# Modulation columns, the first x load, the last z projection and filler products on TensorE, in an AdaLN block of a state-space mixer and a routed transformer layer

## Chip, core and metric

The kernel runs on one core of a Trainium2 chip. The metric is the device time of one execution in microseconds (us); the time before is the median of three runs, 1469.33 us. Engines are named as in the profile: PE is TensorE, ACT is ScalarE, DVE is VectorE, POOL is GpSimd, SP is SyncE, which issues the plain DMAs.

## What is computed

```python
mod = (silu(c) @ wmod).reshape(8, 6, 1, 256)     # sa, ca, ga, sb, cb, gb
h = layernorm(x) * (1 + ca) + sa                 # x: 8 x 1024 x 256
x = x + ga * mixer(h)
h = layernorm(x) * (1 + cb) + sb
x = x + gb * ffn(h)

def mixer(u):                                    # inner width 512, 8 heads, state 64
    x = silu(causal_conv4(u @ Wx.T)); z = u @ Wz.T
    b, c = x @ Wb.T, x @ Wc.T; dt = softplus(x @ Wdt.T + b_dt)
    y = scan(x, b, c, dt, -exp(log_a)) + d * x   # state recurrence over 1024 tokens
    return (groupnorm(y) * silu(z)) @ Wout.T     # z is first needed here

def ffn(x):                                      # 127 of 1024 tokens, picked by a router
    attention (16 heads) and a GELU MLP on the picked tokens, scattered back
```

ga and gb are also clamped away from zero.

## The kernel before, in words

Eight batches run one after the other, all in float32 but for a few bfloat16 operands. Each engine has its own program, written out by hand; it works through it in order and meets the others at semaphores. The mixer of batch b and the routed layer of batch b-1 are interleaved in `batch(b, f)` with f = b-1; the last batch's routed layer (f = 7) follows alone, with nothing to interleave. That stretch, from the end of the last scan to the end of the kernel, is called the tail.

Within a batch PE does: `ln_in` (transposes of the normalised x), `x_proj` and `z_proj` (8 calls each, two halves of 512 tokens by four column blocks, each call two products of 512 columns that the trace shows as 4 records), `bc_proj`, `dt_proj`, then `scan` over eight chunks, whose last product group is `output`. The results go through a ring `proj` of four PSUM banks: job q uses bank q % 4 and waits until job q-4 has been read. `gn_stats`, `out_` and the `ffn_...` steps of batch f stand between them: `ffn_wrow` waits for the router weights `wcol` of DVE, `ffn_rank` for DVE's comparisons, `ffn_idx` for DVE's one-hot rows (`ffn_onehot`), `ffn_turn` for the gathered and normalised tokens, `ffn_AT` for the softmax.

On DVE `out_(f)` (residual, statistics, `wcol`) comes first in a batch, then the convolution in four pieces with `ffn_rank` and `ffn_onehot` between them. On ACT `gn_apply` scales y, `z_silu` writes silu(z), and DVE multiplies the two before PE's `out_` can begin.

At the start SP loads cT and the first 512 columns of wmod, then all of x of batch 0, the rest of wmod and the weights. PE makes row-wise modulation (`modulation(0)`), ACT copies it out, DVE adds 1 to ca, PE turns it into columns (L1489) and ACT copies them into `mcol`; `modulation(1)` and `(2)` follow. The normalised x (ACT L653) waits behind these copies on ACT, and PE's first `x_proj` waits for x and the columns.

The tail on PE before:

```python
output(f, T - 1)
gn_stats(f)
out_(f)
ffn_wrow(f)
ffn_rank(f)
ffn_idx(f)
```

Of the kernel before, what the change touches and what calls it, by code (L numbers as in the profile page):

```python
# [20 lines left out]
ACT = mybir.ActivationFunctionType  # L21
AX = mybir.AxisListType

P = 128
# [19 lines left out]
SD_MOD, SD_MIX, SD_ALL = 10, 12, 16  # L44
# [34 lines left out]
class Ring:  # L79
# [3 lines left out]
    def __init__(self, banks, filled, drained):  # L83
        self.banks, self.filled, self.drained = banks, filled, drained
# [3 lines left out]

    def full(self, b, q):

        return self.filled[q % 4], at(self.filled[q % 4], b, q // 4 + 1)

    def read(self, b, q):

        return self.drained[q % 4], at(self.drained[q % 4], b, q // 4 + 1)


def adaln_block(nc, x, wxT, wzT, wbT, wcT, wdtT, woT, cols, bdt, loga, mask, pos, rw, rb,
                wqkv, wo, w1, w2, lncols, cT, wmod, out):
    ctx = ExitStack()  # L100
    with ctx:
# [175 lines left out]
        mload = ctx.enter_context(nc.semaphore("mod_inputs_loaded"))  # L277
# [86 lines left out]
        def ring(name, banks, jobs):  # L364
            return Ring(banks, [sig(f"{name}_filled{i}", len(range(i, jobs, 4))) for i in range(4)],
                        [sig(f"{name}_drained{i}", len(range(i, jobs, 4))) for i in range(4)])

        proj = ring("proj", ps[0:4], 49)
# [3 lines left out]
        J_X = ((4, 2, 6, 7), (8, 9, 10, 11))  # L372
        J_BC = ((20, 21, 22, 23, 24, 25, 26, 27), (29, 31, 33, 34, 35, 36, 39, 40))
# [8 lines left out]
        def kp(w):  # L382
            return w.rearrange("(k p) n -> p k n", p=P)

        first_loads = ((bdt_s[:, :], bdt), (arow[:, :], loga.partition_broadcast(P)), (cols_s[:, :, :], cols), (wx_s[:, :, :], kp(wxT)),
                       (wz_s[:, :, :], kp(wzT)))
# [7 lines left out]
        def _(sp):  # L394


            sp.dma_start(mcin, cT.rearrange("(k p) n -> p k n", p=P)).then_inc(mload, 16)
            sp.dma_start(wmod_s[:, :, 0:2 * D], kp(wmod)[:, :, 0:2 * D]).then_inc(mload, 16)
            sp.dma_start(xin[:, :, :], x[0, :, :].rearrange("(t p) n -> p t n", p=P)).then_inc(x_loaded, 16)
# [9 lines left out]
            sp.dma_start(mod_d[:, :], mod8).then_inc(mod_stored, 16)  # L409
# [48 lines left out]
        def _(pool):  # L458
# [8 lines left out]
            def ln_in(b, half):  # L467
# [22 lines left out]
                                 base=0, pattern=[[0, 4], [1, P]], channel_multiplier=-1))  # L490
            link(g.memset(ones_b[:, :], 1.0))
# [10 lines left out]
                        allow_small_or_imprecise_dtypes=True))  # L502
            link(g.memset(above[:, :], 0.0))
# [17 lines left out]
            ln_in(0, 0)  # L521
            ln_in(0, 1)
# [113 lines left out]
        def _(act):  # L636
            a = nc.scalar

            act.wait_ge(mload, 16 * 2)
            a.activation(mcin, mcin, ACT.Silu).then_inc(setup_act, 1)  # L640
            act.wait_ge(setup_pe, 1)
            a.activation(mod8[:, 0:2 * D], ps[4][0:NB, :], ACT.Copy).then_inc(setup_act, 1)
            act.wait_ge(setup_pe, 2)
            a.activation(mcol[:, :, :], ps[7][:, 0:4 * NB].rearrange("p (a n) -> p a n", a=4), ACT.Copy
                         ).then_inc(setup_act, 1)
            for j in (1, 2):
                act.wait_ge(setup_pe, j + 2)
                a.activation(mod8[:, 2 * j * D:2 * (j + 1) * D], ps[4 + j][0:NB, :], ACT.Copy).then_inc(setup_act, 1)
# [16 lines left out]
            def gn_apply(b):  # L665
                act.wait_ge(gcoef_ready, at(gcoef_ready, b, 1))
                for half in range(2):
# [38 lines left out]
            def z_silu(b, half, pair):  # L706
                for m in (2 * pair, 2 * pair + 1):
                    q = J_Z + half * KC + m
# [141 lines left out]
            def batch(b, f, last=False):  # L850
                x_copies(b, ((0, (0, 1)),))
                ln_rows(b, 1)
                x_copies(b, ((0, (2, 3)), (1, (0,))))
# [3 lines left out]
                if f is None:  # L857
                    act.wait_ge(mod_stored, 16)
                    act.wait_ge(setup_pool, SP_ALL)
                last_tap(b, 0)  # L860
                z_silu(b, 0, 0)
                z_silu(b, 0, 1)
                last_tap(b, 1)
                z_silu(b, 1, 0)
# [3 lines left out]
                z_silu(b, 1, 1)  # L868
                x_silu(b, 0, 1)
                if f is not None:  # L870
                    second_norm(f)
                bc_copies(b, 0, (0, 1, 2, 3, 4))
# [601 lines left out]
        def _(pe):  # L1474
# [20 lines left out]
            def ln_in(b, half):  # L1495
# [6 lines left out]
                for k in range(KD):  # L1502
                    q = J_H[half][k]
                    if q >= 4:
                        pe.wait_ge(*proj.read(b, q - 4))
# [472 lines left out]
```

## Time and profile before

| | |
|---|---|
| median of 3 runs (lowest, highest) | 1469.33 us (1468.57, 1469.62) |
| the profiled execution, its own time | 1468.33 us |
| its span | 1466.3 us |
| PE busy | 1372.3 us, 94% |
| DVE busy | 996.5 us, 68% |
| ACT busy | 689.5 us, 47% |
| POOL busy | 308.7 us, 21% |
| share of PE in the chain that ended last | 87% |
| mean granted clock of PE | 0.977 |

The span is the profile's own window; the execution's time is 2.0 us more. A busy PE means that matmuls are in flight, not that they run at full speed. The granted clock is 1.00 at 2.4 GHz and 0.50 at 1.2 GHz. The two ends of the kernel are where PE is not busy: over the first 20 us and over the tail, some 115 us long.

### The profile page before, as it was taken

Reading aid. Unit: us, or ns where it says so; the run is one execution under the profiler, and the core shown is the slowest. Engines: PE = TensorE matmul, PEld = TensorE weight load, DVE = VectorE, ACT = ScalarE, POOL = GpSimd, SP = SyncE. Lnnn points to the kernel's source line nnn. Section 1 sums busy time; section 2 is a strip of 40 time slices with the busy share of each in tenths; the row PEclk is TensorE's granted clock in tenths of the full one; section 3 lists DMA queues with packets and bytes.
Section 4 is the critical chain, followed back from the end, with each engine's and each line's share of the span. In section 5 each row is a group of like instructions: output and inputs, shape, how many; then the busy total and the mean of one; then the engine's idle time right before and its main releaser. Section 6 shows DMA issues by size and latency. Waiting matters only on the chain.

```text
span 1466.3 us, 23175 instructions
## 1 busy us (share of the span) xinstructions
PE 1372.3 (94%) x8656; PEld 849.5 (58%) x8656; DVE 996.5 (68%) x2848; ACT 689.5 (47%) x1353; POOL 308.7 (21%) x386
## 2 busy tenths in 40 slices
PE   7999999999999999999999999999999999998434
PEld 2447655676457665576456764576655764567423
DVE  2426797477874787477974778747874779747782
ACT  4434543645445462635436454555626354362212
POOL 3004201241104301142013411043011420133110
PEclk9999999999999999999999999999999999999767
DMA  8001001020000200020010200001000200101010
GB/s 302 6 0 30 15 15 47 3 75 29 25 23 10 68 30 26 22 77 15 15 47 3 76 30 26 22 20 59 29 26 22 77 15 15 47 4 45 29 47 4
DMA packets 47534, 54.24 MB, mean 37 GB/s; under 512 B 7608, under 2 KB 42296, under 8 KB 47424
## 3 DMA queue, kind: packets, MB, share of 16 engines
q1 hardware_dynamic: 41408, 46.42, 9.4%
q0 software_dynamic: 6016, 6.35, 1.7%
q8 instruction: 69, 1.13, 0.3%
q14 instruction: 41, 0.34, 0.1%
HBM read 34.84 MB, written 17.87 MB: 36 GB/s over the span
## 4 chain that ended last, share of the span: by engine, by line
PE 87%; DVE 6%; issue 3%; ACT 1%; DMA 1%; POOL 1%; POOLq 0%; SPq 0%; DVEq 0%; ACTq 0%
PE ps L1519 43%; PE ps L1684 8%; PE ps L1634 5%; PE ps L1593 4%; PE ps L1586 4%; DVE yst L1130 3%; PE ps L1646 2%; PE ps L1605 2%; PE ps L1824 2%; PE ps L1834 2%; PE ps L1620 2%; PE ps L1624 1%; PE ps L1611 1%; PE ps L1789 1%; PE ps L1755 1%
## 5 line engine op out<-in xcount | busy, mean ns | idle before, releaser
L1519 PE MATMUL ps<-xT,wb_s 128*128 128x512 f32 x512 | 230.9, 597 | 0.1
L1519 PE MATMUL ps<-xT,wc_s 128*128 128x512 f32 x512 | 225.4, 593 | 0.0
L1519 PEld LDWEIGHTS ps<-xT,wc_s 128*128 128x128 f32 x512 | 96.1, 190 | 112.3 <-issue 111.9
L1519 PEld LDWEIGHTS ps<-xT,wb_s 128*128 128x128 f32 x512 | 93.6, 190 | 108.4 <-issue 100.9
L1011 DVE SCALAR_TENSOR_TENSOR xT<-xc,cols_s,xT 128x512 f32<-128x512 f32 x192 | 134.8, 748 | 3.2 <-ACT xT L697 0.6
L1519 PE MATMUL ps<-hT,wx_s 128*128 128x512 f32 x256 | 119.0, 609 | 1.9 <-ACT hT L662 1.5
L1684 PE MATMUL ps<-CT,xT 128*128 128x256 f32 x512 | 114.0, 384 | 6.3 <-DVE xT L1190 6.3
L1519 PE MATMUL ps<-hT,wz_s 128*128 128x512 f32 x256 | 112.3, 592 | 0.0
L1684 PEld LDWEIGHTS ps<-CT,xT 128*128 128x128 f32 x512 | 98.7, 193 | 23.2 <-issue 9.8
L729 ACT ACTIVATE BT<-ps 128x512 f32<-128x512 f32 x64 | 37.9, 593 | 151.2 <-PE ps L1519 151.2
L770 ACT ACTIVATE XB<-ps 128x512 f32<-128x512 f32 x64 | 38.4, 599 | 138.3 <-PE ps L1605 138.3
L759 ACT ACTIVATE Eg<-ps 128x512 f32<-128x512 f32 x128 | 72.6, 596 | 53.1 <-PE ps L1624 43.3
L729 ACT ACTIVATE CT<-ps 128x512 f32<-128x512 f32 x64 | 38.1, 595 | 124.3 <-PE ps L1519 124.3
L1113 DVE TENSOR_TENSOR Sbd<-ps,Sdc 64x256 f32<-64x256 f32 x96 | 40.5, 421 | 67.2 <-PE ps L1593 66.5
L603 POOL TENSOR_TENSOR sm<-sm,mhalf 128x1 f32<-128x1 f32 x24 | 14.4, 599 | 324.1 <-DVE sm L1398 307.3
L1099 DVE TENSOR_TENSOR Mt<-ps,Eg 128x512 f32<-128x512 f32 x128 | 82.1, 683 | 0.0
L546 POOL TENSOR_TENSOR EC<-EC,CT 128x512 f32<-128x512 f32 x64 | 79.7, 1272 | 1.3
L1519 PEld LDWEIGHTS ps<-hT,wz_s 128*128 128x128 f32 x256 | 48.1, 190 | 54.9 <-issue 54.5
L1519 PEld LDWEIGHTS ps<-hT,wx_s 128*128 128x128 f32 x256 | 46.9, 192 | 53.3 <-issue 50.6
L552 POOL TENSOR_TENSOR Sdc<-Sbd,dec 128x512 f32<-128x512 f32 x48 | 50.4, 1049 | 127.4 <-DVE Sbd L1113 108.6
L1406 DVE TENSOR_TENSOR ftmp<-ftmp,ps 128x256 f32<-128x256 f32 x8 | 3.4, 420 | 108.6 <-PE ps L1834 108.6
L1634 PE MATMUL ps<-CT,BT 64*128 64x128 f32 x1024 | 74.4, 285 | 1.6 <-ACT EC L749 1.6
(298 smaller groups left out, 2589.0 us busy)
## 6 DMA issues: line engine op xcount, KB each, us to landing
BT<-x SPq DMA_DIRECT2D x8, 1024.0 KB, 5.5
xr<-x SPq DMA_DIRECT2D x8, 1024.0 KB, 9.2
x_scratch<-xr SPq DMA_DIRECT2D x32, 256.0 KB, 2.1
out<-EC SPq DMA_DIRECT2D x32, 256.0 KB, 2.1
modrow<-mod_scratch SPq DMA_DIRECT2D x8, 512.0 KB, 6.8
w_s<-w SPq DMA_DIRECT2D x2, 1024.0 KB, 12.4
xT<-wmod SPq DMA_DIRECT2D x1, 1024.0 KB, 8.6
wb_s<-wbT SPq DMA_DIRECT2D x1, 1024.0 KB, 10.6
```

The lines of the kernel that those rows point to most:

```text
L546: g.tensor_tensor(s, s, CT[:, half, k, :], ALU.mult).then_inc(CE_ready, 1)
L552: g.tensor_tensor(Sdc[:, :, :], Sbd[:, :, :], dec[:, :, c:c + 1].broadcast_to([P, KC, P]), ALU.mult).then_inc(Sdc_ready, 1)
L729: a.activation((BT if m < KC else CT)[:, half, m % KC, :], proj.bank(q)[:, :], ACT.Copy).then_inc(proj.drained[q % 4], 1)
L759: a.activation(Eg[:, s * HALF:(s + 1) * HALF], ps[s][:, :], ACT.Exp).then_inc(Eg_ready, 1)
L1011: ins = v.scalar_tensor_tensor(dst, xcv[:, m, half * HALF + tap:half * HALF + tap + HALF], cols_s[:, m, tap:tap + 1], dst, ALU.mult, ALU.add)
L1099: v.tensor_tensor(Mt[:, c % 2, s * HALF:(s + 1) * HALF], ps[2 + s][:, :], Eg[:, s * HALF:(s + 1) * HALF], ALU.mult).then_inc(Mt_ready, 1)
L1130: ins = v.bn_stats(yst[:, k, 6 * part:6 * part + 6], xT[:, k, first * P:end * P])
L1519: ins = t_.matmul(bank[:, :], w[:, k, m * P:(m + 1) * P], rhs[:, k, half * HALF:(half + 1) * HALF], start=k == 0, stop=k == nk - 1)
L1586: t_.matmul(ps[4][:, k * P:(k + 1) * P], Sbd[:, k, :], ECv[:, k, c * P:(c + 1) * P], start=k == 0, stop=True, skip_group_check=k > 0)
L1593: ins = t_.matmul(ps[4][64 * hh:64 * hh + 64, k * P:(k + 1) * P], XB[:, c % 2, 0, h * STATE:(h + 1) * STATE], Mt[:, c % 2, hh * HALF + k * ...
L1634: ins = t_.matmul(ps[2 + s][:, k * P:(k + 1) * P], BT[r, c // 4, k, chunk(c)], CT[r, c // 4, k, chunk(c)], start=True, stop=True)
L1684: ins = t_.matmul(ps[4 + j][:, i * D:(i + 1) * D], xT[:, k, t * P:(t + 1) * P], wog_s[:, k, :], start=k == 0, stop=k == KC - 1)
```

## The change

There are four edits. At the start, x's first half (512 KB) is the first load and x's second half comes after wmod's first part; the modulation columns are made by PE directly in column form and read by DVE, and `modulation(1)` and `(2)` move behind the fourth `x_proj` call; the exponential of log_a on ACT moves behind the `x_copies`; POOL's two `ln_in` stand earlier in its setup. In the last batch (b = 7) all eight `z_proj` calls move behind the scan, around `gn_stats`, into ring jobs 49 to 56; ACT's `z_silu` for them stands around `gn_apply`. In the tail ACT does `ffn_wrow` ahead of `second_norm`. And `keep_busy(n)` puts n products of 512 bfloat16 columns that nobody reads into a bank of PSUM: 17 at the start, 122 in the tail.

```diff
+            sp.dma_start(xin[:, 0:4, :], x[0, 0:HALF, :].rearrange("(t p) n -> p t n", p=P)).then_inc(xhead, 16)
+            sp.dma_start(mcin, cT.rearrange("(k p) n -> p k n", p=P)).then_inc(cload, 16)
             sp.dma_start(wmod_s[:, :, 0:2 * D], kp(wmod)[:, :, 0:2 * D]).then_inc(mload, 16)
-            sp.dma_start(xin[:, :, :], x[0, :, :].rearrange("(t p) n -> p t n", p=P)).then_inc(x_loaded, 16)
+            sp.dma_start(arow[:, :], loga.partition_broadcast(P)).then_inc(aload, 16)
+            sp.dma_start(xin[:, 4:T, :], x[0, HALF:L, :].rearrange("(t p) n -> p t n", p=P)).then_inc(x_loaded, 16)
+            sp.dma_start(wx_s[:, :, :], kp(wxT)).then_inc(wxload, 16)
             sp.dma_start(wmod_s[:, :, 2 * D:], kp(wmod)[:, :, 2 * D:]).then_inc(mload2, 16)
...
-            pe.wait_ge(mload, 32)
-            pe.wait_ge(setup_act, 1)
-            modulation(0)
-            pe.wait_ge(setup_dve, 1)
-            pe.wait_ge(setup_pool, 2)
-            for j in range(4):
-                ins = t_.transpose(ps[7][:, j * NB:(j + 1) * NB], mod8[:, j * P:(j + 1) * P], ident[0:NB, 0:NB])
-            ins.then_inc(setup_pe, 1)
-            pe.wait_ge(mload2, 16)
-            modulation(1)
-            modulation(2)
+            def mod_columns():
+                pe.wait_ge(mload, 16)
+                pe.wait_ge(setup_act, 1)
+                for j in range(4):
+                    for k in range(KD):
+                        ins = t_.matmul(ps[7][:, j * NB:(j + 1) * NB], wmod_s[:, k, j * P:(j + 1) * P],
+                                        mcin[:, k, :], start=k == 0, stop=k == KD - 1)
+                ins.then_inc(setup_pe, 1)
+
+            def keep_busy(n, bank=ps[0]):
+                for _ in range(n):
+                    t_.matmul(bank[:, :], identb[:, :], causal[:, :, :].rearrange("p a n -> p (a n)"),
+                              start=True, stop=True)
...
+            pe.wait_ge(setup_pool, 9)
+            keep_busy(8, ps[3])
+            mod_columns()
+            keep_busy(6, ps[3])
+            ln_in(0, 0)
+            keep_busy(3, ps[3])
             batch(0, None)
...
             output(f, T - 1)
+            pe.wait_ge(Eg_ready, at(Eg_ready, f, 2 * T))
+            pe.wait_ge(Mt_ready, at(Mt_ready, f, 2 * T))
+            z_proj(f, 0, range(3))
             gn_stats(f)
+            z_proj(f, 0, (3,))
+            z_proj(f, 1, range(4))
             out_(f)
+            keep_busy(12)
             ffn_wrow(f)
+            keep_busy(36)
             ffn_rank(f)
+            keep_busy(6)
             ffn_idx(f)
+            keep_busy(30)
             pe.wait_ge(hn_ready, at(hn_ready, f, 1))
...
             ffn_qT(f)
+            keep_busy(8)
             ffn_scores(f)
+            keep_busy(24)
             ffn_AT(f)
             ffn_av(f)
             ffn_wo(f)
+            keep_busy(6)
             pe.wait_ge(hnb_ready, at(hnb_ready, f, 1))
...
-            gn_apply(f)
+            z_silu(f, 0, 0)
+            z_silu(f, 0, 1)
+            z_silu(f, 1, 0)
+            gn_apply(f, (0,))
+            z_silu(f, 1, 1)
+            gn_apply(f, (1,))
+            ffn_wrow(f)
             second_norm(f)
-            ffn_wrow(f)
```

PE at the very start, before (L1478 is `modulation`, L1489 the turn into columns, L1507 `ln_in`, L1519 `x_proj`):

```order
L1478 MATMUL ps<-xT,mcin_s 8x512 x2
L1489 MATMUL ps<-ident,CT 128x8 x4
L1478 MATMUL ps<-xT,mcin_s 8x512 x4
L1507 MATMUL ps<-ident,BT 128x128 x8
L1519 MATMUL ps<-hT,wx_s 128x512 x4
```

and in the change (L1531 is `keep_busy`, L1524 `mod_columns`, L1551 `ln_in`, L1563 the projections, L1514 `modulation`):

```order
L1531 MATMUL ps<-causal,identb 128x512 x8
L1524 MATMUL ps<-mcin_s,xT 128x8 x8
L1531 MATMUL ps<-causal,identb 128x512 x6
L1551 MATMUL ps<-ident,BT 128x128 x8
L1531 MATMUL ps<-causal,identb 128x512 x3
L1563 MATMUL ps<-hT,wx_s 128x512 x4
L1551 MATMUL ps<-ident,BT 128x128 x8
L1563 MATMUL ps<-hT,wx_s 128x512 x4
L1514 MATMUL ps<-xT,mcin_s 8x512 x4
```

The four wide row products have moved from ahead of the first projection to between its calls. PE in the last batch, before, from `out_` (L1684) on:

```order
L1684 MATMUL ps<-CT,xT 128x256 x32
L1519 MATMUL ps<-hT,wz_s 128x512 x12
L1696 MATMUL ps<-ident,wcol 128x128 x8
L1519 MATMUL ps<-hT,wz_s 128x512 x4
L1519 MATMUL ps<-xT,wb_s 128x512 x12
```

and in the change (L1729 is `out_`, L1741 `ffn_wrow`):

```order
L1729 MATMUL ps<-CT,xT 128x256 x32
L1741 MATMUL ps<-ident,wcol 128x128 x8
L1563 MATMUL ps<-xT,wb_s 128x512 x12
```

The 16 z products (32 records) are gone from between `out_` and `bc_proj`. PE in the tail, where they went, around `gn_stats` (L1718), with the last `output` (L1637) ahead:

```order
L1637 MATMUL ps<-Mt,XB 64x128 x8
L1563 MATMUL ps<-hT,wz_s 128x512 x6
L1718 MATMUL ps<-pk,halfmean 128x8
L1563 MATMUL ps<-hT,wz_s 128x512 x10
L1729 MATMUL ps<-CT,xT 128x256 x32
L1531 MATMUL ps<-causal,identb 128x512 x12
L1741 MATMUL ps<-ident,wcol 128x128 x8
L1531 MATMUL ps<-causal,identb 128x512 x36
```

Six z products now stand ahead of `gn_stats` and ten behind it.

## Rows read from the trace of the kernel before

**Rows 1.** Timeline of the first 50 us: start, us, engine, line, operation

```profile
0.81 0.43 SPq L397 DMA_DIRECT2D mcin_s<-cT  x1
...
3.57 0.64 POOL L489 TENSOR_SCALAR_AFFINE_SELECT causal<-causal 128x512 bf16<-128x512 bf16 x1
...
5.72 3.46 PE L1478 MATMUL ps<-xT,mcin_s 128*8 128x512 f32 x4 [5.72 <-ACT mcin_s L640]
...
10.15 1.41 DVE L948 BATCH_NORM_STATS2 st<-BT 128x6 f32<-128x256 f32 x4
...
10.90 3.60 PE L1478 MATMUL ps<-xT,mcin_s 128*8 128x512 f32 x8 [0.32 <-DMA xT<-wmod]
...
13.82 0.20 POOL L476 TENSOR_TENSOR mrs<-mrs,negone 128x4 f32<-128x4 f32 x1
...
15.03 2.06 ACT L653 ACTIVATE BT<-BT,mrs,rstd 128x256 f32<-128x256 f32 x4
...
17.14 1.09 PE L1507 MATMUL ps<-ident,BT 128*128 128x128 f32 x8 [2.64 <-ACT BT L653]
...
19.45 5.23 PE L1519 MATMUL ps<-hT,wx_s 128*128 128x512 f32 x8 [1.21 <-ACT hT L662]
...
35.84 13.90 PE L1519 MATMUL ps<-hT,wz_s 128*128 128x512 f32 x32
```

**Rows 2.** PE's timeline, last batch and tail; idle before, releaser in brackets

```profile
1211.64 10.46 PE L1519 MATMUL ps<-hT,wz_s 128*128 128x512 f32 x24
...
1241.25 0.34 PE L1717 MATMUL ps<-tok,Mt 128*128 128x2 bf16 x8
...
1352.20 1.09 PE L1593 MATMUL ps<-Mt,XB 128*64 128x128 f32 x16
...
1397.78 0.53 PE L1707 MATMUL ps<-ones_b,EC 128*128 128x1 bf16 x14 [9.96 <-DVE Mt L1255]
...
1411.37 0.69 PE L1725 MATMUL ps<-ident,ftmp 128*128 128x128 f32 x2 [10.09 <-DVE ftmp L1314]
```

**Rows 3.** Windows of 2 us: lengths, busy time by engine, then granted clock (PEclk)

```profile
1356.00:1358.00 2.00, 0.00 (x0) 0.00 (x0) 1.93 (x8) 0.00 (x0) 0.00 (x0) 0.80 0.01 4
...
1370.00:1372.00 2.00, 2.00 (x9) 1.64 (x8) 0.14 (x1) 0.00 (x0) 0.00 (x0) 0.79 0.00 0
```

**Rows 4.** DMA issues of the first 60 us: KB, us to landing

```profile
xT<-wmod SPq DMA_DIRECT2D x1, 512.0 KB, 4.0
```

**Rows 5.** The chain that ended last: start, us, engine, tile, line

```profile
1199.93 11.87 PE ps L1684 x55
...
1300.41 3.72 PE ps L1824 x32
...
1313.31 0.43 PE ps L1620 x2
...
1359.59 0.61 PE ps L1673 x2
...
1366.54 16.20 PE ps L1684 x64
...
1442.94 5.28 PE ps L1824 x32
```

**Rows 6.** DVE's timeline in the last batch

```profile
1215.82 8.54 DVE L1011 SCALAR_TENSOR_TENSOR xT<-xc,cols_s,xT 128x512 f32<-128x512 f32 x12
1225.13 2.19 DVE L1246 SCALAR_TENSOR_TENSOR Mt<-Eg,wcol,tri 128x128 f32<-128x128 f32 x8 [0.77 <-ACT Eg L787]
...
1234.12 4.31 DVE L1011 SCALAR_TENSOR_TENSOR xT<-xc,cols_s,xT 128x512 f32<-128x512 f32 x6
...
1238.74 1.66 DVE L1267 TENSOR_SCALAR Mt<-iota_r,rank 128x128 f32<-128x128 f32 x8
```

**Rows 7.** ACT's timeline in the tail

```profile
1362.74 5.76 ACT L670 ACTIVATE xT<-xT,gab 128x512 f32<-128x512 f32 x8 [15.16 <-DVE gab L1184]
...
1387.55 1.05 ACT L787 ACTIVATE Eg<-ps 128x512 f32<-128x512 f32 x2
```

More of the change, by code:

```diff
@@ L361, in adaln_block, with ring @@
         scattered = sig("scattered", 16)
-        def ring(name, banks, jobs):
+        def ring(name, banks, jobs, short=0):
             return Ring(banks, [sig(f"{name}_filled{i}", len(range(i, jobs, 4))) for i in range(4)],
-                        [sig(f"{name}_drained{i}", len(range(i, jobs, 4))) for i in range(4)])
-        proj = ring("proj", ps[0:4], 49)
+                        [sig(f"{name}_drained{i}", len(range(i, jobs, 4))) for i in range(4)], short)
+        proj = ring("proj", ps[0:4], 49, short=20)
         ffn = ring("ffn", ps[4:8], 26)
@@ L372, in adaln_block, with z_job @@
         J_X = ((4, 2, 6, 7), (8, 9, 10, 11))
+        J_Z_LAST = J_EC + 8
+        def z_job(b, half, m):
+            return (J_Z_LAST if b == NB - 1 else J_Z) + half * KC + m
         J_BC = ((20, 21, 22, 23, 24, 25, 26, 27), (29, 31, 33, 34, 35, 36, 39, 40))
@@ L637, in _, with mod_rest @@
             a = nc.scalar
-            act.wait_ge(mload, 16 * 2)
+            act.wait_ge(cload, 16)
             a.activation(mcin, mcin, ACT.Silu).then_inc(setup_act, 1)
[L641 to L648, printed above, removed]
+            def mod_rest():
+                for j in (1, 2):
+                    act.wait_ge(setup_pe, j + 1)
+                    a.activation(mod8[:, 2 * j * D:2 * (j + 1) * D], ps[4 + j][0:NB, :], ACT.Copy
+                                 ).then_inc(setup_act, 1)
             def ln_apply(b, half):
@@ L663, in ln_rows, with gn_apply @@
                                  bias=mc[:, k:k + 1], scale=mc[:, 2 + k:3 + k]).then_inc(proj.drained[q % 4], 1)
-            def gn_apply(b):
+            def gn_apply(b, halves=(0, 1)):
                 act.wait_ge(gcoef_ready, at(gcoef_ready, b, 1))
-                for half in range(2):
+                for half in halves:
                     for k in range(KC):
@@ L857, in batch @@
                 if f is None:
-                    act.wait_ge(mod_stored, 16)
-                    act.wait_ge(setup_pool, SP_ALL)
+                    act.wait_ge(wload, 16 * len(first_loads))
+                    act.wait_ge(aload, 16)
+                    a.activation(arow[:, :], arow[:, :], ACT.Exp).then_inc(setup_act, 1)
                 last_tap(b, 0)
-                z_silu(b, 0, 0)
-                z_silu(b, 0, 1)
+                if not last:
+                    z_silu(b, 0, 0)
+                if not last:
+                    z_silu(b, 0, 1)
                 last_tap(b, 1)
-                z_silu(b, 1, 0)
+                if not last:
+                    z_silu(b, 1, 0)
                 x_silu(b, 0, 0)
@@ L867, in batch @@
                     ffn_wrow(f)
-                z_silu(b, 1, 1)
+                if not last:
+                    z_silu(b, 1, 1)
                 x_silu(b, 0, 1)
@@ L945, in ln_stats @@
             def ln_stats(b, tiles):
-                dve.wait_ge(x_loaded, at(x_loaded, b, 16))
+                if not later(b):
+                    dve.wait_ge(xhead, 16)
+                if later(b) or tiles[0] >= 4:
+                    dve.wait_ge(x_loaded, at(x_loaded, b, 16))
                 for t in tiles:
@@ L1512, in project @@
                 if q >= 4:
[L1513 removed]
+                    pe.wait_ge(*proj.prev(b, q))
                 bank = proj.bank(q)
```

94 lines of the change are left out of this document (57 added, 37 removed).

## The prediction, made before the changed kernel was run

> **What bounds the kernel now.** I read the timeline of the first 50 us first [rows 1]. PE waits there for x and for the modulation columns: it starts the first x projection at 19.45 and is then dense for the rest of batch 0. That first group of 8 records takes 5.23 us; at the pace of the z projections (32 records in 13.90, so 0.434 each and 1.74 a call) it would take 3.5. So the clock was low there, and it is worth 1.8 us. In the middle PE is the bound, and 87% of the chain that ended last is PE. Then I read PE's timeline with its idle times [rows 2]: in the tail PE stands still before nearly every group, 9.96 us before the rank products and 10.09 before the first transposes of the gathered rows. The 2-us windows show the granted clock falling from 1.00 to 0.50 (2.4 to 1.2 GHz) around 1357, four microseconds after PE's last product of the scan ended at 1353.3, and rising only around 1371, four microseconds after it became dense again [rows 2, 3].
>
> **Start.** The first load is now 512 KB of x. The nearest row is 512 KB of wmod, landed 4.0 us after its issue [rows 4]; issued at 0.81 [rows 1], x's half lands at 4.8. From the first statistics (10.15) to the end of mrs (14.02) is 3.87 us, so ACT can normalise at 8.7; its four take 2.06, and from their end (17.10) to the first projection (19.45) there were 2.35 [rows 1]. That path gives 13.1. The other path is PE's own: fillers may start when the causal mask is made, 4.2. A filler has the form of the two in 0.43 us [rows 5], so 0.216 at 2.4 GHz and 0.43 at 1.2. PE's first four records took 3.46 in all, 0.86 each, and the next eight 3.60, 0.45 each [rows 1]: the clock starts low and has risen by 10.9. I take 8 fillers at 0.43 (to 7.7), then the 8 column products. They show as 16 records; the nearest rows are 32 records with 128 columns in 3.72 warm [rows 5], 0.116 each, so 1.9 us, or 3.7 at half clock; I take 2.5, as the clock should rise on the way. Six fillers at 0.216 end at 11.5, and transposes, ACT's two copies and a high clock take 2.0 more: 13.5. Bounds for this start: 13.1 (the ACT path) and 16.3 (columns and six fillers wholly at 1.2 GHz: 7.7+3.7+2.6, plus the 2.35 of before). I take 13.5.
>
> From there to the end of the z projections: 16 calls, half of each kind, at 1.74 (27.8), 8 transposes (0.9), and now the 8 records of `modulation` as well (3.6, [rows 1]; before they lay in the wait ahead of the start). That is 32.3, so 45.8; before it was 49.74. **Gain 3.9 us.** DMA issues and the log_a exponential with its table load (some 1.5 us on ACT behind the x copies, hidden under z projections before PE needs the first xT) I cost at 0; if that cover is short, it costs up to 0.6. The late store of the modulation rows is waited for by ACT only before the B copies, when 15 us have passed: 0.
>
> The Trainium skill, "TensorE: Matmul & The Clock Gate", section "Back-to-back issue gap", gives about 131 ns per product of 512 columns in a sustained stream; the row shows 216 for this form. By the page the six fillers would end 0.5 us sooner and the gain at the start would be 4.3, not 3.9; I go by the row.
>
> **Last batch.** 32 records, 13.9 us of PE, leave a dense stretch, but what follows needs DVE. Before, z ran from 1211.64 and the index products came at 1241.25 [rows 2]. DVE finishes `wcol` just before the convolution starts at 1215.82 [rows 6]; PE, done with `out_` at 1211.7, now waits 4.1 for it. The B projection needs xT, so the convolution: its first six operations end at 1220.1, plus ACT 0.6, and the second six at 1224.4, plus 0.6. So PE starts at 1220.7, waits again until 1225.0 in the middle of the first call, and does three calls by about 1233.8 (8 records of 0.434 each, 3.47). DVE's rank compare started at 1225.13 after a wait of 0.77 for ACT's copy of wrow; this wait goes, as ACT copies it at 1221. Everything on DVE comes 0.77 sooner, the last one-hot row at 1240.40-0.77 = 1239.6 [rows 6]. PE, through with the fourth B call at 1238, waits for it, then runs the index products at 1239.65 instead of 1241.25. **Gain 1.6 us** of 13.9; some 12 go into four new waits. If the clock is low after these waits, one call costs 1.7 more, and the last wait (1.6) covers it. The rest of the batch follows with PE and DVE in step and keeps the 1.6. Bounds 0.8 (only DVE's part) and 3.
>
> **Tail.** z call by call: three from 1353.3 (end of the last `output`, [rows 2]) to 1358.5, still ahead of `gn_stats` at 1359.59 [rows 5]. Then five: the second of them after the one for half 0, so z(1,1), ends at 1365.0, its silu at 1365.6. ACT's `gn_apply` started at 1362.74 [rows 7], now it waits behind that silu: 2.9 later, and with it `out_`. But the clock stays up: `out_` took 16.20 for 64 records, and at 0.216 a record (55 in 11.87) it takes 13.8 [rows 5], 2.4 less. Sum +0.5. ACT's wrow copies ahead of the second norm: they started at 1387.55 [rows 7], behind four tiles of the second norm; PE's transposes alone allowed them some 0.3 sooner, an estimate, -0.3. Fillers: 12, 36, 6 and 30 take 2.6, 7.8, 1.3 and 6.5 at 0.216, in a gap of 4.1 (as from `out_` to `wcol` in the last batch), 9.96, the 1.66 of the one-hot rows [rows 6] and 10.09: hidden. The groups behind them run at 2.4 GHz: 32 records of w1 took 5.28 and take 3.72 warm [rows 5], -1.6. The rank, index and transpose groups are short (the first rank rows are 14 in 0.53, [rows 2]): half of about 1.5 us, -0.7, an estimate between 0 and -1.3. From the gathered rows to the end of the softmax DVE is dense, so nothing else there counts. **Gain 2.1 us**, bounds -1 (z delays not repaid by the clock) and 3.5.
>
> **Sum.** 3.9+1.6+2.1 = 7.6. The profiled execution took 1468.33 (span 1466.3): 1460.7. The median of the runs is 1.0 higher, so 1461.7.
>
> **Rivals.** (a) The clock is low through the columns and the first projections, as it was for the first 8 records: start at 16.3, gain 1.1 there, in all 4.8, time 1464.5. For it speaks that the very first products ran at half; against, that PE is now busy from 4.2 on without a break. (b) The z move doesn't do what it is meant to: the last batch gives back nothing, as DVE's own chain holds it, and the tail loses the 2.9 without the 2.4: 7.6-1.6-2.4 = 3.6, time 1465.7. For it: 24 us of DVE work between `wcol` and the last one-hot row, 1215.8 to 1240.4, that nothing shortens; against: the 0.77 and PE's own lag of 1.0 behind the one-hot rows. (c) More is gained: the start at 13.1 with the waits of the last batch shorter and clocked high (bound 3) and the tail at its 3.5: 7.6+0.4+1.4+1.4 = 10.8, time 1458.5. (d) Slower: the fillers run at 1.2 GHz. 36 take 15.5 in the 9.96 before the rank products (+5.5), 30 take 12.9 in 10.09 (+2.8), and the gains of the high clock (1.6+0.7) are lost: 7.6-10.6 = -3.0, time 1472.3. It begins to cost when one filler takes over 0.277 (9.96/36), and decides against the change when they add more than 5.3 beside the 2.3 lost. Against: at the end of `out_` the clock was 1.00 in the trace, and the pause there is now 1.2 us where a fall took four [rows 3].
>
> For (d) the Trainium skill has a rule, in the same page, section "A second HAM failure mode: psum-queue depth-cycling": small idle times between groups of matmuls can make the clock go back and forth. The trace does not bear it out: the clock held for four microseconds of full idleness after 1353.3.
>
> **How the numbers follow.** Chances: forecast 0.50, (a) 0.16, (b) 0.14, (c) 0.12, (d) 0.08, counting under (d) milder forms. A measurement of this kernel can tell 0.2%, 2.9 us, from no change. The forecast, (a) and (c) are faster; (b) at 3.6 is just so, and I put three parts in ten of it, with one quarter of (d), at no change, and give 0.05 more to errors that I don't see: faster 0.85, same 0.10, slower 0.05. The range takes in the forecast (1459.5 to 1463.5 by itself), (a), most of (b), and (c) down to where half of it lies: 1458.0 to 1466.3.
>
> **What would show it.** First x projection at 13 to 14 in 3.5 us, not 5.2; bc projections of batch 0 from 46. In the last batch idle on PE before wrow, twice in the first B call and before the index products, 12 us in all, and DVE with no gap before the rank compare. In the tail `gn_apply` behind the third pair of silus, a granted clock of 1.00 from the scan to the rank products, and w1 in 3.7. I am wrong if PE's idle before the rank products is nil (fillers on the path), if ACT's order at the start delays xT, or if the column products take 6 us.

## The result, and the profile after

| kernel | median us | runs | lowest to highest |
| --- | --- | --- | --- |
| before | 1469.6 | 20 | 1467.5 to 1475.4 |
| changed | 1466.2 | 20 | 1463.5 to 1471.1 |

The changed kernel takes 0.9979 of the time before (95% interval 0.9971 to 0.9987): 3.1 us faster by this ratio, 3.4 by the medians, and not the 7.6 of the prediction. Its profiled execution took 1465.4 (span 1463.4), against 1468.3 before.

Below, an offset is the start of a place less the start of the same place in the first profile of the kernel before; a negative one is earlier. In the profiled execution the start came out as forecast. PE's timeline of the changed kernel, first 48 us; L1531 are the unread products, L1524 the modulation columns:

```profile
4.26 3.59 PE L1531 MATMUL ps<-causal,identb 128*128 128x512 bf16 x8 [4.26 <-POOL causal L509]
7.64 2.26 PE L1524 MATMUL ps<-mcin_s,xT 128*128 128x8 f32 x16
9.76 1.46 PE L1531 MATMUL ps<-causal,identb 128*128 128x512 bf16 x6
...
13.63 3.67 PE L1563 MATMUL ps<-hT,wx_s 128*128 128x512 f32 x8 [0.89 <-ACT hT L680]
...
32.18 14.23 PE L1563 MATMUL ps<-hT,wz_s 128*128 128x512 f32 x32
```

The first x projection starts at 13.63 in place of 19.45 [rows 1] and the bc projections at 46.25 in place of 49.57: 3.3 sooner. The first eight unread products took 0.45 each (half clock), the next six 0.24.

Some 60 us later, at the scan start of batch 0, 1.3 us of this is gone. PE's timeline before (first two rows), then after; they wait equally long for ACT:

```profile
109.89 1.77 PE L1574 MATMUL ps<-xc,spread 128*128 128x512 bf16 x4 [0.19 <-ACT EC L749]
113.22 1.16 PE L1634 MATMUL ps<-CT,BT 64*128 64x128 f32 x16 [1.57 <-ACT EC L749]
```

```profile
109.91 1.21 PE L1678 MATMUL ps<-CT,BT 64*128 64x128 f32 x16 [1.57 <-ACT EC L767]
111.05 1.03 PE L1664 MATMUL ps<-causal,identb 128*128 128x512 bf16 x2
112.02 0.61 PE L1668 MATMUL ps<-xc,Lw 64*128 64x512 bf16 x2
```

Windows of the changed kernel there; the granted clock is the third number from the end (before it was 1.00 in all of them):

```profile
108.00:110.00 2.00, 0.43 (x3) 0.14 (x3) 0.00 (x0) 1.86 (x4) 1.89 (x3) 1.00 0.00 0
110.00:112.00 2.00, 2.00 (x18) 1.01 (x18) 0.00 (x0) 0.00 (x0) 2.00 (x2) 0.72 0.03 8
112.00:114.00 2.00, 2.00 (x10) 1.55 (x10) 0.00 (x0) 1.34 (x3) 1.27 (x2) 0.50 0.00 0
```

The same idle times were followed by a low clock in the one execution and not in the other. Another 0.35 goes in batch 1, where DVE stands still between two score tiles for no wait that the profile shows ("issue"). From there to batch 7 the offset stays at -1.65 or -1.66.

```profile
251.20 0.69 DVE L1408 SCALAR_TENSOR_TENSOR EC<-ps,Sbd 128x508 f32<-128x508 f32 x1 [0.27 <-issue]
```

Last batch, PE's timeline after:

```profile
1214.16 1.97 PE L1741 MATMUL ps<-ident,wcol 128*128 128x128 f32 x8 [4.01 <-DVE wcol L1246]
1219.28 3.75 PE L1563 MATMUL ps<-xT,wb_s 128*128 128x512 f32 x4 [3.16 <-ACT xT L722]
1223.42 8.94 PE L1563 MATMUL ps<-xT,wb_s 128*128 128x512 f32 x20 [0.38 <-ACT xT L722]
...
1237.94 0.35 PE L1762 MATMUL ps<-tok,Mt 128*128 128x2 bf16 x8 [1.16 <-DVE Mt L1303]
```

The four waits are where they were expected, 8.7 us in all. Of the other 5.2 of the 13.9 moved, 1.65 was gained, and most of the remaining 3.5 went into products at half clock (eight wrow records in 1.97, before 1.04; four B records in 3.75, warm 1.88). DVE's rank compare follows the convolution without a gap, as forecast. The index products stand at 1237.94 against 1241.25 [rows 2]: 3.31, less the 1.66 brought along, is 1.65.

The tail, PE's timeline after:

```profile
1349.91 5.42 PE L1563 MATMUL ps<-hT,wz_s 128*128 128x512 f32 x12
...
1366.25 14.05 PE L1729 MATMUL ps<-CT,xT 128*128 128x256 f32 x64 [0.89 <-DVE xT L1226]
...
1395.26 0.50 PE L1752 MATMUL ps<-ones_b,EC 128*128 128x1 bf16 x14 [2.09 <-DVE Mt L1291]
...
1408.77 0.69 PE L1770 MATMUL ps<-ident,ftmp 128*128 128x128 f32 x2 [3.59 <-DVE ftmp L1350]
1409.37 1.97 PE L1781 MATMUL ps<-ident,Mt 128*128 128x128 f32 x8
1411.13 4.57 PE L1800 MATMUL ps<-wqkv_s,ftmp 128*128 128x512 f32 x8
...
1431.18 3.71 PE L1834 MATMUL ps<-ident,EC 128*127 128x128 f32 x16 [4.11 <-DVE EC L1421]
...
1441.51 3.84 PE L1869 MATMUL ps<-ftmp,w_s 128*128 128x128 f32 x32 [0.47 <-ACT ftmp L857]
```

Measured from the offset of -3.31, `out_` (L1729) comes 3.0 later, needs 14.05 for 16.20 [rows 5], and the rank products (L1752) come 0.79 later. Then 3.59 of idle are left behind the 30 unread products, the granted clock falls from 0.99 to 0.50, and it is still low in the query/key/value products (L1800), for which DVE waits:

```profile
1406.00:1408.00 2.00, 0.00 (x0) 0.00 (x0) 1.86 (x8) 0.00 (x0) 0.42 (x1) 0.99 0.02 4
1408.00:1410.00 2.00, 1.23 (x5) 0.92 (x6) 1.73 (x4) 0.38 (x1) 0.25 (x1) 0.50 0.00 0
```

```profile
1414.79 0.69 DVE L1381 COPY qkrt<-ps 128x512 f32<-128x512 f32 x1 [0.77 <-PE ps L1800]
```

That copy had no wait before, and the eight records it waits for took 3.49 there for 4.57 here:

```profile
1413.74 3.49 PE L1755 MATMUL ps<-wqkv_s,ftmp 128*128 128x512 f32 x8
```

w1 (L1869, the first products of the MLP), 3.84 for 5.28, gives 1.4 back. From the group-norm product to the end of the span the tail took 107.1 us, before 106.7.

### The profile page after: what moved, and what is told of

The parts are those of the page before. It is cut to its first block, busy times and chain, and to the rows that moved or that the text cites. A ratio compares the mean times of both kernels' runs of the same rounds, so it can differ in the third digit from the quotient of the medians.

```text
span 1463.4 us, 23472 instructions
## 1 busy us (share of the span) xinstructions
PE 1403.8 (96%) x8803; PEld 862.6 (59%) x8803; DVE 996.6 (68%) x2849; ACT 689.1 (47%) x1351; POOL 308.5 (21%) x386
## 4 chain that ended last, share of the span: by engine, by line
PE 85%; DVE 8%; issue 4%; ACT 1%; POOL 1%; DMA 0%; POOLq 0%; SPq 0%; DVEq 0%
PE ps L1563 41%; PE ps L1729 8%; PE ps L1678 5%; PE ps L1637 4%; PE ps L1630 4%; DVE yst L1166 3%; PE ps L1690 2%; PE ps L1649 2%; PE ps L1869 2%; PE ps L1879 2%; PE ps L1664 2%; PE ps L1655 2%; PE ps L1668 1%; PE ps L1834 1%; PE ps L1800 1%
## 5 line engine op out<-in xcount | busy, mean ns | idle before, releaser
L1563 PE MATMUL ps<-xT,wb_s 128*128 128x512 f32 x512 | 232.9, 601 | 3.6 <-ACT xT L722 3.5
L1563 PE MATMUL ps<-xT,wc_s 128*128 128x512 f32 x512 | 225.4, 593 | 0.0
L1563 PEld LDWEIGHTS ps<-xT,wc_s 128*128 128x128 f32 x512 | 96.1, 190 | 112.3 <-issue 111.9
L1563 PEld LDWEIGHTS ps<-xT,wb_s 128*128 128x128 f32 x512 | 94.1, 191 | 113.1 <-issue 104.5
L1563 PE MATMUL ps<-hT,wx_s 128*128 128x512 f32 x256 | 117.7, 603 | 1.6 <-ACT hT L680 1.2
L1563 PE MATMUL ps<-hT,wz_s 128*128 128x512 f32 x256 | 112.8, 593 | 0.1
L1729 PE MATMUL ps<-CT,xT 128*128 128x256 f32 x512 | 111.9, 379 | 0.9 <-DVE xT L1226 0.9
L1729 PEld LDWEIGHTS ps<-CT,xT 128*128 128x128 f32 x512 | 97.2, 190 | 17.8 <-issue 5.0
L1563 PEld LDWEIGHTS ps<-hT,wz_s 128*128 128x128 f32 x256 | 47.9, 190 | 55.4 <-issue 54.2
L1563 PEld LDWEIGHTS ps<-hT,wx_s 128*128 128x128 f32 x256 | 46.1, 190 | 52.7 <-issue 50.0
```

Source lines behind the costliest of these rows:

```text
L1563: ins = t_.matmul(bank[:, :], w[:, k, m * P:(m + 1) * P], rhs[:, k, half * HALF:(half + 1) * HALF], start=k == 0, stop=k == nk - 1)
L1729: ins = t_.matmul(ps[4 + j][:, i * D:(i + 1) * D], xT[:, k, t * P:(t + 1) * P], wog_s[:, k, :], start=k == 0, stop=k == KC - 1)
```

## Experiments

Medians of several runs; each group (e1, e2, e3) has a chip of its own, and the median of before is that of the same chip. The interval is that of the ratio to before. Across groups compare the gains against before: the changed kernel's is 3.4 by the medians, 3.1 by the ratio.

| kernel | us | before | ratio (95%) |
| --- | --- | --- | --- |
| e1_start_only | 1469.8 | 1470.4 | 0.9997 (0.9988 to 1.0006) |
| e1_z_home | 1468.0 | 1470.4 | 0.9984 (0.9973 to 0.9995) |
| e1_no_tail_fill | 1468.2 | 1470.4 | 0.9985 (0.9975 to 0.9995) |
| e1_no_start_fill | 1466.6 | 1470.4 | 0.9974 (0.9964 to 0.9984) |
| e2_longer_fill | 1465.2 | 1470.0 | 0.9965 (0.9951 to 0.9979) |
| e2_batch0_fill | 1465.6 | 1470.0 | 0.9969 (0.9958 to 0.9980) |
| e2_half_z | 1464.8 | 1470.0 | 0.9966 (0.9953 to 0.9980) |
| e2_all | 1461.1 | 1470.0 | 0.9938 (0.9924 to 0.9951) |
| e3_before_filled | 1464.8 | 1469.5 | 0.9966 (0.9953 to 0.9978) |
| e3_all_z_home | 1461.0 | 1469.5 | 0.9948 (0.9934 to 0.9962) |
| e3_all_no_start_fill | 1461.6 | 1469.5 | 0.9947 (0.9934 to 0.9961) |
| e3_all_early_fill | 1458.8 | 1469.5 | 0.9928 (0.9914 to 0.9942) |

### The parts of the change, one at a time

**e1_start_only** leaves the last batch and the tail as they were:

```diff
-            z_proj(f, 0, range(3))
             gn_stats(f)
...
-            keep_busy(36)
```

> Only the start edits (columns made directly, first x half first, 17 unread products at the start); the z projections of the last batch, the wcol order and the tail are those of the kernel before. Theory A (the start gives what the two traces show, 3.3 us at the first bc projection, and a granted clock that falls at the scan start of batch 0 takes up to 1.3 to 1.65 of it back in some executions): 1469.6 - 3.3 = 1466.3 where the clock stays, about 1468 where it falls. Theory B (the start's gain is made up by later waits, and the z move is what the changed kernel gains from): 1469.3 to 1469.6. The prediction's term for the start was 3.9, which would be 1465.7.

Measured 1469.8, no gain: theory B's number. But its trace shows the gain at the bc projections, 46.35, and loses it at places that A named only in part: 1.3 at batch 0 and 0.35 in batch 1, as A has it, and then 3.6 in the tail, which took 110.3 us instead of 106.7 with the same code. The last group below asks why.

**e1_z_home** puts the z products back:

```diff
-                if b < NB - 1:
-                    z_proj(b, 0, range(4))
-                    z_proj(b, 1, range(2))
+                z_proj(b, 0, range(4))
+                z_proj(b, 1, range(2))
```

> The changed kernel with the 32 z products of the last batch back in that batch; start edits, wcol order and all unread products stay. Theory A (the move gives 1.65 in the last batch and costs 3.0 - 2.15 = 0.85 at the first output projection, since the z products end after the group-norm coefficients): the kernel is as fast as the changed one within 1 us, 1465.4 to 1467.0. Theory B (the move is what hurts the tail, and without it the prediction's terms of 3.9 start, 0.3 wcol order, 1.6 w1 and 0.7 small groups would hold): 1463.1. Theory C (all of the gain comes from the move): 1469.

Measured 1468.0: theory B falls; A's upper end and C's number are both 1.0 away. Against before of its chip it gains 2.4, 1.0 less than the changed kernel (0.7 by the ratios, whose intervals overlap), which fits A. Its trace shows what the move does: the offset of -1.88 goes through the last batch unchanged, where each of the five traces with the full move gains 1.64 or 1.65. Its tail took 108.0 in spite of the unread products; the clock was 0.50 from 1432 to 1444.

**e1_no_tail_fill** removes the seven groups of unread products of the tail (one shown), **e1_no_start_fill** the three of the start:

```diff
-            keep_busy(30)
```

> The changed kernel without the 122 unread products of the tail. Theory A (they gave 1.43 at the w1 products and the first rows after the output projection, little elsewhere): 1.4 to 2.5 us slower than the changed kernel, 1467.6 to 1468.7. Theory B (they only move the low clock from a hidden stretch into the query/key/value products, where VectorE waits for it): the same or up to 0.5 faster, 1465.7 to 1466.2.

> The changed kernel without the 17 unread products of the start. Theory A (they hold the clock for the first x projections, whose 8 products take 3.67 with it and took 5.23 without): about 1.5 us slower than the changed kernel, 1467.7. Theory B (the clock has risen by then anyway from the modulation columns and transposes): no difference, 1466.2. A third way: the granted clock's fall at the scan start of batch 0 depends on when the waits there fall, so that a shift of 1 us takes it away, and the kernel is as fast or faster though its start is later.

1468.2 is within A's range for the tail, but against before of its chip the loss is 1.3 by the medians and 0.9 by the ratios, a little under A's 1.4; its tail took 108.9, 1.8 more than the changed kernel's. For the start, 1466.6: theory A's 1.5 is not there in the median (gain 3.7, against 3.4). In its trace the first x projection starts at 14.17 but takes 6.33, and the bc projections stand at 49.46, 3.2 later than in the changed kernel; the clock did not fall at batch 0 (third way), which returned 1.3, and its tail was 106.0.

### Holding the clock

**e2_longer_fill** and **e2_batch0_fill**:

```diff
-            keep_busy(36)
+            keep_busy(45)
...
-            keep_busy(30)
+            keep_busy(46)
...
-            keep_busy(24)
+            keep_busy(42)
```

> The changed kernel with its three long groups of unread products in the tail lengthened to what the idle left behind them holds (36 to 45, 30 to 46, 24 to 42; idle left was 2.09, 3.59 and 4.11 us). Theory A (the tail of the changed kernel is late because the granted clock falls in the idle that these groups leave, so that the transposes, masks and query/key/value products run at half rate): the clock stays high to the end of the tail; query/key/value products 3.5 instead of 4.57, transposes of the attention rows about 2 to 3.1 instead of 3.71; 1.0 to 2.5 us faster than the changed kernel, 1463.7 to 1465.2, and less scatter. Theory B (unread products hold up the real ones, which wait behind them on TensorE): the same or slower, 1466.2 to 1467.5.

```diff
                 carry_rows(b, 0)
+                if f is None:
+                    keep_busy(1, ps[4])
...
                 carry_rows(b, 1)
+                if f is None:
+                    keep_busy(6, ps[4])
```

> The changed kernel with 7 more unread products in batch 0, one between the two halves of the carry rows and six in the wait before the first scores (1.57 us). Theory A (the fall of the granted clock there, 1.3 us of the start's 3.3, comes from the idle before the scores and is kept away by filling it): the offset at the first x projection of batch 1 against the kernel before is -3.3 instead of -2.0, and the whole is 1.3 us faster in those executions in which the clock fell, 0.5 to 1.3 in the median, 1464.9 to 1465.7. Theory B (the clock falls there by when in the program the start has put the waits, whatever is in them): no change, 1466.2, with the clock still falling at 110 us.

In the first the clock is 1.00 through the tail up to PE's last product (two of the windows):

```profile
1402.00:1410.00 8.00, 7.90 (x37) 3.38 (x35) 4.71 (x17) 0.00 (x0) 4.80 (x7) 1.00 0.40 116
1410.00:1418.00 8.00, 6.17 (x34) 4.33 (x34) 7.52 (x22) 1.04 (x4) 0.00 (x0) 1.00 0.00 0
```

The tail took 105.7 instead of 107.1, 1.4 less, as A said, and the median's gain against before, 4.9, is some 1.4 more as well. In the second, the windows of batch 0 that were 0.72 and 0.50 (the stretch lies 2.6 later here, and the window from 114 to 116 reads 1.00 too):

```profile
110.00:112.00 2.00, 1.80 (x8) 0.70 (x8) 0.00 (x0) 2.00 (x6) 1.25 (x2) 1.00 0.00 0
112.00:114.00 2.00, 1.73 (x20) 1.09 (x18) 0.00 (x0) 0.49 (x2) 2.00 (x3) 1.00 0.03 8
```

The offset of its late start, -0.68 at the bc projections, is still -0.67 in batch 1: nothing is lost, and 1465.6 is in A's range. But e2_longer_fill, started equally late (48.89), also kept 0.68 there without these products, so this pair of traces doesn't decide. All 18 profiles together say more. What went at batch 0, by whether the seven products stood there:

| profiles | without the seven | with the seven |
| --- | --- | --- |
| bc projections 1.2 to 3.5 us ahead of before's | 5 of 6 lost 1.3 to 1.5 | 0 of 4 lost any |
| the others (0.7 ahead to 4.9 behind) | 0 of 6 | 0 of 2 |

In the five the clock fell at that place. So no filled execution lost the clock there and most early unfilled ones did; not each needs the filling.

**e2_half_z** moves only half of the z products (16 of the trace's 32 records), with 22 unread ones behind them:

```diff
+                z_proj(b, 0, range(4))
                 if b < NB - 1:
-                    z_proj(b, 0, range(4))
...
-            z_proj(f, 0, range(3))
+            z_proj(f, 1, range(3))
             gn_stats(f)
-            z_proj(f, 0, (3,))
-            z_proj(f, 1, range(4))
+            z_proj(f, 1, (3,))
+            keep_busy(22, ps[6])
```

> The changed kernel with only the second half of the last batch's z products (16 of 32, 7.0 us) behind the scan, the first half back in its place, and 22 unread products behind them. Theory A (VectorE's rank and one-hot work bounds the last batch's start, so that 16 moved products give the same 1.65 there as 32; and with 16 the first output projection no longer waits for z, which costs the changed kernel 3.0 us): the last batch's index products at the same offset of -1.65 from the batch's start, the first output projection 3.0 earlier, total 2.5 to 3.3 faster than the changed kernel, 1463 to 1463.7. Theory B (the 32 were needed: with 16 less idle, TensorE bounds again): the last batch gives less, 0 to 0.8, and the whole 0 to 2 faster.

> All three edits of this group together. Theory A: their parts add, 1.0 to 2.5 for the held clock in the tail, 0.5 to 1.3 for batch 0 and 2.5 to 3.3 for the half move: 4.0 to 6.5 faster than the changed kernel, 1459.7 to 1462.2, and with less scatter than either kernel. Theory B (the clock's state in the tail is what all of the differences come from, one high stretch for another low one): 1463.5 to 1466.

In the trace of e2_half_z the last batch gives 1.46 (1.45 to 1.65 in the four traces of the half move), and `out_` starts 3.2 before its old time instead of 0.3: that is theory A. The profiled execution took 1461.8, but the median, 1464.8, is only 1.3 below the changed kernel's (1.7 by the gains against before), outside A's range and in B's for the whole. The runs lie in two groups: six took 1460.8 to 1464.8, at a mean granted clock of 0.989 to 0.991, and five 1466.8 to 1468.2, at 0.987 or 0.988. With all three edits, e2_all, the clock is 1.00 from 1340 to 1450, and 1461.1 is 5.1 below the changed kernel (5.5 by the gains), in A's range, and more than the three medians by themselves add to (1.0, 0.6 and 1.3). In e2_all the last batch gave 1.65, from -0.92 to -2.57. PE's timeline of its tail, `out_` in the last row:

```profile
1350.65 5.42 PE L1558 MATMUL ps<-hT,wz_s 128*128 128x512 f32 x12
1357.03 0.39 PE L1713 MATMUL ps<-pk,halfmean 128*128 128x8 f32 x2 [0.96 <-DVE pk L1205]
1357.28 1.96 PE L1558 MATMUL ps<-hT,wz_s 128*128 128x512 f32 x4
1359.08 4.91 PE L1526 MATMUL ps<-causal,identb 128*128 128x512 bf16 x22
1363.83 4.49 PE L1724 MATMUL ps<-CT,xT 128*128 128x256 f32 x20
```

### What each part is worth with the clock held

> The kernel before with unread products alone: 7 at the scan start of batch 0, 24 ahead of the group-norm product of the tail, 28 behind it, and then 12, 45, 6, 46, 8, 42 and 6 in the places where the changed kernel has its groups. No start edits, z in place, wcol order as before. Theory A (most of what is to be had in the tail is the clock: from the group-norm product to the end the kernel before took 106.7 us, and with z delayed by 3.0 but the clock held it took 105.7, so 102.7 without that delay): 4.0 faster than before, 1465.6 at a median of before of 1469.6, more where before's clock was worse. Theory B (the clock's low stretches are hidden behind VectorE and ScalarE): 0 to 1.5 faster, 1468 to 1469.6.

> The kernel with all three edits (half z, longer groups, batch 0), but with all z products back in the last batch, and 24 and 28 unread products where the z products stood in the tail. Theory A (the move itself is worth the 1.65 seen in the last batch, in every trace with it): 1.65 slower, 1462.7. Theory B (the move's worth was the held clock in the tail, which the unread products now hold as well, and the 1.65 comes back as a wait): the same, 1461.1.

> The kernel with all three edits, without the 17 unread products of the start. Theory A (with the first products earlier the clock rises earlier; the profiled starts of the first x projection were 13.5 to 16.3 with them, and its 8 products took 3.67 each time, and 14.17 with 6.33 without): 0 to 3 slower, 1462.6 in the middle. Theory B (the groups at the start delay as much as they gain, since they run at the low clock in front of the modulation columns and the transposes): 1461.1, the same, as the changed kernel with and without them differed by only 0.5.

> The kernel with all three edits, whose first group of 8 unread products (from 4.26 us on, when GpSimd's mask is ready) is replaced by 15 of a tile that VectorE clears at the start, so that TensorE begins at about 1.3 us. Theory A (the clock rises a time after TensorE has begun that varies from execution to execution, and the start's scatter of 2.7 us is that): the modulation columns are already at the high clock in most executions, the first x projection at 13.5 in the profile, 1 us faster in the median, 1460, with less scatter. Theory B (the scatter of the start is that of the transfers): no change, 1461.1.

**e3_before_filled** gains 4.7 with unread products alone (theory A), more than the whole change did. Its tail took 102.3 us, 4.4 less than before, though its profiled start was late (x projection at 23.82). **e3_all_z_home** has the start edits and the wcol order besides: 3.9 faster by medians and 2.6 by the ratios, whose intervals overlap. Its median, 1461.0, is theory B's number; by the ratios it is 1.5 slower than e2_all (0.9948 against 0.9938), near A's, and the intervals overlap. The traces tell more: 1.65 in the last batch with the move, 0.00 without (offset -3.20 before and after), 0.3 given back in the tail (101.9 against 102.2). So by the traces the move is worth about 1.4, which five or six runs of either can't resolve. **e3_all_no_start_fill** is 0.5 slower than e2_all by the medians, 1.3 by the ratios, within scatter: what the unread products are worth where the change places them is not resolved. **e3_all_early_fill** begins them 3 us sooner:

```diff
+            v.memset(warm[:, :], 0.0).then_inc(warm_ready, 1)
...
+            pe.wait_ge(warm_ready, 1)
+            for _ in range(15):
+                t_.matmul(ps[3][:, :], warm[:, 0:P], warm[:, :], start=True, stop=True)
+            mod_columns()
             pe.wait_ge(setup_pool, 9)
-            keep_busy(8, ps[3])
-            mod_columns()
```

It is the best kernel of the study: 1458.8, 10.7 below before, all five runs between 1458.5 and 1459.6. Theory A's start is there (x projection at 13.53; e2_half_z, with the old first group, had that too), and the median is 1.2 better than A's; 0.35 of that is what this build doesn't lose in batch 1. PE's timeline of its start, and below it that of e2_longer_fill, whose clock rose late:

```profile
1.26 5.15 PE L1964 MATMUL ps<-warm 128*128 128x512 bf16 x15 [1.26 <-DVE warm L1000]
6.32 1.95 PE L1522 MATMUL ps<-mcin_s,xT 128*128 128x8 f32 x16
8.12 1.46 PE L1529 MATMUL ps<-causal,identb 128*128 128x512 bf16 x6
```

```profile
7.64 3.42 PE L1524 MATMUL ps<-mcin_s,xT 128*128 128x8 f32 x16
10.92 2.72 PE L1531 MATMUL ps<-causal,identb 128*128 128x512 bf16 x6
13.43 1.91 PE L1551 MATMUL ps<-ident,BT 128*128 128x128 f32 x8
```

### Does the tail's time belong to the kernel or to the execution?

> The kernel before, profiled again. If the tail's time belongs to the execution, its tail (group-norm product to the end) and its start differ from the first profile's 106.7 and 19.45 by microseconds, and the granted clock falls at other places in it. If it belongs to the kernel, the tail is 106.7 within 0.3.

> The kernel before, profiled once more, with the same two expectations as the run ahead of it: another tail than 106.7 and other places of the clock, or 106.7 within 0.3.

> The kernel with the start edits alone, profiled again. If the tail's time belongs to the execution: anything from 106 to 111 us. If it belongs to the kernel: 110.3 within 0.3, and 3.2 of the start's gain is always lost there.

> The kernel with the start edits alone, once more, with the same two expectations: a tail of anything from 106 to 111 us, or 110.3 within 0.3.

| profile | bc projections | group-norm product | span | tail |
| --- | --- | --- | --- | --- |
| before | 49.57 | 1359.59 | 1466.3 | 106.7 |
| e4_before_a | 49.91 | 1359.92 | 1466.9 | 107.0 |
| e4_before_b | 51.01 | 1361.02 | 1470.2 | 109.2 |
| e1_start_only | 46.35 | 1358.02 | 1468.3 | 110.3 |
| e4_start_only_a | 48.93 | 1359.29 | 1468.8 | 109.5 |
| e4_start_only_b | 46.69 | 1358.56 | 1465.4 | 106.8 |

It belongs to the execution: each kernel has short tails and long ones, and the places of the low clock differ. Most of the difference lies between the transposes of the gathered rows and w1. This stretch took 31.6 us in the three short tails and 34.0 in the three long ones, where the clock stayed at 0.50 through the attention products; in all six profiles whose waits are filled to the end it took 31.3. In e4_start_only_b it was 1.00 by the attention product, in e4_before_b 0.50 up to w1 (rows of the one, then of the other):

```profile
1436.13 1.08 PE L1838 MATMUL ps<-EC,ftmp 127*32 127x128 f32 x32 [0.79 <-ACT EC L846]
1437.79 1.10 PE L1848 MATMUL ps<-fwo_s,ftmp 128*128 128x256 f32 x4 [0.58 <-ACT ftmp L852]
```

```profile
1438.88 1.94 PE L1802 MATMUL ps<-EC,ftmp 127*32 127x128 f32 x32 [0.78 <-ACT EC L828]
1441.40 2.05 PE L1812 MATMUL ps<-fwo_s,ftmp 128*128 128x256 f32 x4 [0.59 <-ACT ftmp L834]
```

The mean granted clock of each run carries this over to the runs without a trace. Of the 12 runs of e1_start_only 9 have a mean of 0.974 or less, and of the 34 of before on that chip 9; its other three (0.975 to 0.978) took 1466.9 to 1468.2, while the 17 of before at 0.976 or 0.977 took 1467.8 to 1470.3. So at a like clock the start's gain is seen, though on three runs only, and in the median it goes to executions with more low clock. In the changed kernel too the six slowest of the 20 runs, 1468.8 to 1471.1, have 0.984 to 0.986, and no run at 0.988 or more took over 1467.6. Why the start edits alone bring more of these executions stays open.

## Why the prediction was right and wrong

Against the profiled execution the sum said 1460.7, and 1465.4 came: 4.7 too little; against the medians 1461.7, and 1466.2 came. A gain of 7.6 was forecast, and less than half of it was there. By its steps:

- **Start, first x projection at 13.5**: right in this execution, 13.63, and 3.67 for the group. Columns 2.26 for 2.5. The execution was an early one, which is luck: in the eleven profiles with this start it stood at 13.4 to 16.3, 14.6 in the middle, and in four of them the columns took 3.42 and the six products behind them 2.72, which is rival (a)'s slow start.
- **Gain 3.9 us at the end of z**: 3.3 in the trace. The ACT part costed at 0 cost 0.3: the table load and exponential of log_a stand at 33.0 in front of the last taps, and z took 14.23 for 13.90 (one wait of PE for ACT's reading of a bank). That is within the bound given (0.6). Another 0.2 is a reading: the sum measures from 49.74, the modelled end of z, where the bc projections start at 49.57.
- **The start's gain carried unchanged to the sum**: failed. The sum took it over 1300 us as it was; the trace lost 1.3 at batch 0 to the clock and 0.35 in batch 1. Neither place is named in the prediction. None of the six profiles with that stretch filled loses anything at batch 0. The cause of the 0.35 stays open.
- **Last batch, gain 1.6**: right, 1.65, and by the path named. The waits were 8.7 us, not 12; products at half clock took the place of the rest, and a last wait of 1.16 was still left behind them, as the prediction has it. Half of the move gives nearly the same (1.45 to 1.65).
- **Tail, z against clock, +0.5**: 0.9. z delays `out_` by 3.0 (2.9), the clock returns 2.15 (2.4).
- **wcol order, -0.3**: -0.1 (the rank compare is at +0.80, the wrow products at +0.89, against the offset).
- **w1, -1.6**: right, -1.4.
- **Rank, index and transpose groups, -0.7, "nothing else there counts"**: the step that failed most. From the rank products to the transposes of the gathered rows the gain was 0.1. The fillers behind the index products left 3.6 us idle, the clock fell after them instead of long before, and the query/key/value products, for which DVE had no wait before, came 0.8 too late for it; the attention transposes (3.71, before 3.35) added 0.3 and what follows kept it. Tail in all: 0.4 lost, 2.1 forecast. Where the waits are filled to the end (e2_longer_fill) the 0.8 and the 0.3 are gone: the stretch from the transposes to w1 takes 31.3 us, against 32.7 in the changed kernel and 31.6 in the profile of before. But from the rank products to the transposes the gain is 0.1 there too, so at most 0.4 of the 0.7 was to be had against that profile, and its tail, 105.7, is 1.0 shorter than before's, not 2.1; the z delay and the wcol order are the rest. In the long tails the same stretch had 2.7 us to give (34.0), which the single profile didn't show.

So 0.6 of the 4.7 lies in the start, 1.65 in what was lost behind it and 2.5 in the tail. The median is inside the range by 0.1 (1466.3), through rival (b) (1465.7), and that is luck, as (b)'s mechanism isn't what happened: the last batch gave its share and the clock of `out_` did repay most of the delay. Rival (d), unread products at half clock in the tail, didn't occur in the profile (36 in 7.93, 30 in 6.63). The prediction read the clock in one execution as a fixed property of the kernel: "the pause there is now 1.2 us where a fall took four" was right for that place, and the same reading of the idle of batch 0 (0.19 and 1.57, clock 1.00 before) would have found it safe, which it was not.

The Trainium skill, page "TensorE: Matmul & The Clock Gate", section "What's actually happening", says that the number of slow products at a kernel's start differs from run to run of the same kernel. The traces agree: with the same code up to there, the 16 column records of the kernels with the start edits and the first group from 4.26 on took between 1.85 and 3.42 us in eleven traces. The same page, section "A second HAM failure mode: psum-queue depth-cycling", has small idle times make the clock go back and forth. The prediction set it aside for the waits of the tail; batch 0 of the changed kernel, 0.72 and 0.50 after waits of 0.19 and 1.57, speaks for it, and seven of the twelve traces with that stretch unfilled, where the clock stayed at 1.00, show that it isn't so each time.

## What to carry to other kernels

Where TensorE has waits of microseconds, its clock in a single profile is one draw: take several, and compare stretch by stretch, before giving a term of the sum to it. The mean granted clock of each run helps to tell whether the profiled one is typical. Fill such waits to the end: half-filled ones moved the low clock here to where another engine waits (32.7 us in a stretch that takes 31.3), though they were still better than none (tail 107.1, without them 108.9). Filling alone gave 4.7 us here, and starting it at 1.3 us, with whatever is ready first, another 2.3 against e2_all and 2.9 against e3_all_no_start_fill, on the same chip.

## What was not expected of the hardware

- The same tail code takes 106.7 to 110.3 us in six profiles, by where the granted clock is 0.50; with unread products in its waits and the clock at 1.00 it takes 102.3 (e3_before_filled).
- Waits of 0.19 and 1.57 us in a stretch otherwise busy can be followed by a fall of the clock (0.72, 0.50; five of twelve traces), or not (1.00; seven).
- In the first microseconds the granted clock reads 1.00 while products of 512 columns take 0.45 us each, 0.22 to 0.24 later: only the durations tell the state there.
- DVE stood still for 0.27 us ("issue") at one place of batch 1 in the changed kernel, and 0.35 us go there in 13 of the 14 traces with the start edits, not in that of e3_all_early_fill, which has the same instructions there, and in none of the kernel before.
